# Maxima of a pair six units ahead of its exponentials instead of seven

## The reference

```python
q = (x @ Wq).reshape(B, S, 2 * H, d) * scaling      # d = 4, 2 * H = 32
scores = einsum('bhqd,bhkd->bhqk', q, k)            # causal mask, softmax over k
attn_weights = probs[:, :, 0] - lam * probs[:, :, 1]
attn = einsum('bhqk,bhkd->bhqd', attn_weights, v)   # RMS norm per head, times rms_w
x = layernorm(x + attn @ Wo)
r = sigmoid(xr @ W_r.T);  k = relu(xk @ W_k.T) ** 2 # xr, xk mix x with the row before
x = layernorm(x + r * (k @ W_v.T))
```

## Time and profile before

| | |
|---|---|
| time, median of 3 runs | 441.94 us (440.62 to 442.19) |
| profiled execution, its own time | 441.16 us |
| its span in the trace | 439.4 us |
| mean granted clock of TensorE | 0.965 |
| busy, share of the span | TensorE 90%, VectorE 90%, ScalarE 80%, GpSimd 51% |

### The profile page before, as it was taken

The page is one execution under the profiler, slowest core; times in us unless marked ns, Lnnn a source line. Parts: engine busy times, 40 slices in busy tenths (PEclk is TensorE's granted clock), DMA queues, the critical chain, the costliest instruction groups (busy, mean ns, idle before and its releaser), DMA issues.

```text
span 439.4 us, 16522 instructions
## 1 busy us (share of the span) xinstructions
PE 395.6 (90%) x5720; PEld 186.5 (42%) x5721; DVE 397.3 (90%) x565; ACT 350.9 (80%) x732; POOL 225.2 (51%) x514
## 2 busy tenths in 40 slices
PE   5846999999999999999999999999999999999882
PEld 3512444444444444444444444444444444445552
DVE  1889999999999999999999999999999999773854
ACT  2520799999999999999999999999999999787143
POOL 7300132565656565656565656565656565558412
PEclk9975599999999999999999999999999999999998
DMA  5564254321121111111111111111111110000011
GB/s 141 177 215 145 90 194 148 98 51 51 51 53 48 48 48 48 48 48 48 48 48 49 48 48 49 48 48 48 48 48 48 48 50 28 26 3 1 1 49 48
DMA packets 21390, 28.44 MB, mean 65 GB/s; under 512 B 4960, under 2 KB 9952, under 8 KB 21232
## 3 DMA queue, kind: packets, MB, share of 16 engines
q1 hardware_dynamic: 20768, 27.58, 20.9%
q10 hardware_dynamic: 592, 0.46, 0.3%
HBM read 20.39 MB, written 9.47 MB: 68 GB/s over the span
## 4 chain that ended last, share of the span: by engine, by line
PE 60%; DVE 13%; ACT 12%; issue 9%; DMA 2%; SPq 1%; POOL 1%; ACTq 1%; DVEq 0%; POOLq 0%
PE acc L677 26%; PE mx L595 13%; DVE part_max L1133 10%; ACT e_buf L1028 10%; PE ex L647 8%; PE ex L685 3%; PE mx L604 2%; PE ex L631 1%; SPq L316 1%; DMA x_tok<-in_L_attn_x 1%; PE mx L814 1%; PE mx L769 1%; PE mx L677 1%; PE ex L696 1%; POOL rs L545 1%
## 5 line engine op out<-in xcount | busy, mean ns | idle before, releaser
L1133 DVE TENSOR_REDUCE part_max<-mx 128x2 f32<-128x1024 f32 (+2 forms) x288 | 334.8, 1211 | 6.3 <-PE mx L595 2.3
L1028 ACT ACTIVATE e_buf<-ex 128x512 f32<-128x512 f32 x576 | 306.2, 601 | 36.5 <-PE ex L647 30.7
L516 POOL TENSOR_SCALAR_AFFINE_SELECT e_buf<-e_buf 128x256 f32<-128x256 f32 x256 | 100.7, 411 | 168.9 <-ACT e_buf L1028 168.7
L677 PE MATMUL acc<-e_buf,v_grp 128*32 128x256 f32 x2756 | 181.5, 352 | 4.1 <-issue 2.5
L647 PE MATMUL ex<-qe,ke 26*128 26x512 bf16 (+3 forms) x768 | 144.7, 333 | 0.7 <-ACT e_buf L1028 0.6
L595 PE MATMUL mx<-km,qm 29*128 29x128 bf16 (+3 forms) x1280 | 116.9, 270 | 12.8 <-DVE part_max L1133 10.0
L595 PEld LDWEIGHTS mx<-km,qm 26*128 26x128 bf16 (+1 forms) x1280 | 41.7, 93 | 113.8 <-DVE part_max L1133 73.5
L677 PEld LDWEIGHTS acc<-e_buf,v_grp 128*32 128x32 f32 x2756 | 64.8, 109 | 55.8 <-issue 35.5
L647 PEld LDWEIGHTS ex<-qe,ke 26*128 26x128 bf16 x768 | 45.4, 91 | 20.7 <-ACT e_buf L1028 8.2
L499 POOL TENSOR_TENSOR r_rms<-sq_eps,minus_half 128x16 f32<-128x16 f32 x15 | 43.7, 2912 | 0.1
L604 PE MATMUL mx<-mask,pick 32*128 32x128 bf16 x512 | 25.8, 220 | 0.0
(11 more groups left out here) (137 smaller groups left out, 253.6 us busy)
## 6 DMA issues: line engine op xcount, KB each, us to landing
qm<-q_rows SPq DMA_DIRECT2D x32, 128.0 KB, 2.5
km<-k_rows SPq DMA_DIRECT2D x32, 128.0 KB, 2.7
qe<-q_rows SPq DMA_DIRECT2D x32, 128.0 KB, 2.5
ke<-k_rows SPq DMA_DIRECT2D x32, 128.0 KB, 2.7
q_rows<-part_q SPq DMA_DIRECT2D x6, 256.0 KB, 3.0
k_rows<-part_k SPq DMA_DIRECT2D x6, 256.0 KB, 3.3
q_rows<-part_q SPq DMA_DIRECT2D x6, 192.0 KB
k_rows<-part_k SPq DMA_DIRECT2D x6, 192.0 KB
```

Of the source, the lines that this page charges most:

```text
L516: pool.affine_select(out=e, in_=e, compare_op=ALU.is_ge, fill=0.0, base=0, pattern=[[0, PAIR], [1, P]], channel_multiplier=-1)\
L677: last = pe.matmul(out, v, e, start=first, stop=over, skip_group_check=True)
L1028: nc.scalar.activation(e_buf[:, b, i, :], ex[:, ex_slot(b, i) % EX_BANKS, :], ACT.Exp).then_inc(s["exped"], 1)
L1133: nc.vector.tensor_reduce(target, mx_of(n, pr, m)[:].rearrange("p s (a b) -> p s a b", a=a), AX.X, ALU.max).then_inc(s["maxed"], 1)
```

## The change

The maxima of a pair begin six units ahead of its exponentials instead of seven: burst b goes with unit b + 6. The prologue does 15 units instead of 16. The transposes of the maxima move with it by one burst, from behind burst 5 to behind burst 6, in the prologue from unit `NU + 3` to `NU + 2`. In the last group the first transpose of attn, which waits for the last unit, moves from behind burst 1 to behind burst 2, on TensorE and on ScalarE. Through `m = b + EARLY`, VectorE combines at burst 3 and splits at burst 4.

```diff
-EARLY = 7
+EARLY = 6
-TAKE_AT, TURN_AT, MAXIMA_AT, INVERT_AT = 3, 7, 5, 2
+TAKE_AT, TURN_AT, MAXIMA_AT, INVERT_AT = 3, 7, 6, 2
@@ TensorE
-                if u == NU + 3:
+                if u == NU + 2:
                     turn_maxima(0, 2)
-            beside = {(0, 1): [(turn_attn, 0)], (0, 2): [(turn_attn, 1)], (0, 3): [(project, 0)],
+            beside = {(0, 2): [(turn_attn, 0), (turn_attn, 1)], (0, 3): [(project, 0)],
@@ ScalarE
-            beside = {(0, 1): [(copy_attn, 0)], (0, 2): [(copy_attn, 1)], (0, 8): [(copy_x1, 0)],
+            beside = {(0, 2): [(copy_attn, 0), (copy_attn, 1)], (0, 8): [(copy_x1, 0)],
```

## The result

The changed kernel takes 436.53 us (median of 4 runs, 436.37 to 437.08) against 442.06 us (440.62 to 442.37) for the kernel before on the same chip: a ratio of 0.9883, interval 0.987 to 0.9896. That is 5.5 us or 1.2% faster.

What follows compares the result with a forecast made beforehand. The prediction took VectorE to bind, a TensorE-ScalarE loop close behind; -0.9 (tail) + 0.2 (start) - 0.7 (transpose) + 0 (split) = -1.4 us, from the 441.94 us median to 440.5 us. The range ran from 438.0 to 446.0 us.

Steps and rivals of the forecast that it cites:

- VectorE turns only part of it into time: Loop: of some 0.2 us a pair of slack, VectorE gives back at most 1.4 us; half taken, -0.7 us.
- What bounds the kernel: Loop: VectorE binds, busy 43.35 of 43.77 us per four pairs, with a loop through TensorE and ScalarE close behind.
- Part 1: Stream of maxima: same 288 units on VectorE; if fed, the last still ends at 377.69 us, with 15 bursts left behind.
- Part 2: Tail: burst 2 done while TensorE waits for VectorE, attn's transposes side by side; -0.9 us, bounds 0 and -1.1.
- Part 3: Start: burst 0 follows prologue unit 15 instead of 16, perhaps one more burst at slow clock; +0.2 us.
- Part 4: Maxima's transpose behind burst 6: ring order gives some 0.2 us a pair of slack; -0.7 us, bounds -1.4 and +4.3.
- Part 5: Rows of maxima: DMAs land 2.5 us after first issue, a 0.05 us wait at burst 0 inside slack; bound 21 us.
- the estimated 18 us: Rows of maxima: cost if the DMA's fixed 2.0 us counted from the issue's end, about 0.6 us a pair.
- Part 6: Reciprocal behind unit 8 on VectorE: long split meets GpSimd's chain elsewhere, up to 0.27 us either way in 15 pairs; 0 taken.
- the loop relaxes and the split comes clear: Rival, 20 in 100: VectorE's waits for TensorE go (-1.4 us), long splits halve (-2 us); with tail -4 us, 438 us.
- The late maxima: Rival, 13 in 100: TensorE waits at burst 0 of each pair for the maxima's landing; +5 us (447 us) to +15 us.
- the starved VectorE: Rival, 9 in 100: transposes in two neighbouring bursts take TensorE beyond VectorE's pace; +3.4 us, 445 us.

Runs made afterwards that it cites:

- e5: Kernel before with GpSimd's normalisation of a group behind burst 7 instead of burst 2, last group unchanged: 440.78 us, ratio 0.9981.
- e8: Kernel before with VectorE's reciprocal behind burst 1 (unit 8) instead of burst 2: 440.91 us, ratio 0.9985.
- e2: Kernel before with only the first transpose of attn and its copy moved from behind burst 1 to behind burst 2: 439.72 us, ratio 0.9962.
- e1: Kernel before, lead of seven units kept, with the maxima's transpose behind burst 6 instead of 5: 447.58 us, ratio 1.0132.
- e15: Changed kernel with both attn transposes and copies behind burst 3 instead of 2, and GpSimd's normalisation behind burst 7: 437.54 us, ratio 0.9901.
- e4: Changed kernel, lead of six units kept, with the maxima's transpose back behind burst 5: 444.67 us, ratio 1.0067.
- e16: Kernel before with reciprocal behind unit 8, maxima's transpose behind the sums of burst 5, and GpSimd's normalisation behind burst 7: 439.54 us, ratio 0.9952.
- e9: Changed kernel with VectorE's reciprocal behind the combination again (burst 3 instead of burst 2): 438.91 us, ratio 0.9944.

## Why the prediction was wrong

The sum was -0.9 (tail) + 0.2 (start) - 0.7 (transpose and ring) + 0 (split) = -1.4 us. The trace shows -0.86 - 0.05 - 3.69 = -4.6 us. The step that failed is the one that capped the steady part: "VectorE turns only part of it into time", with half of 1.4 us taken and nothing for the split. Its parts in order.

**What bounds the kernel: wrong in its last step.** "VectorE binds, with a loop through TensorE and ScalarE close behind it" took for one limit what is several. I read the busy share: 43.35 of 43.77 us. But e5 took 3.1 us of splits from VectorE and the kernel gained 1.0, and e8 took VectorE out of the chain at 43.73 us a turn. A busy share of 99% didn't show the bound: most of what was taken from it came back inside the engine's own busy time.

**Part 1, the stream of maxima: wrong in its end.** The same 288 units begin at 24.51 us for 24.59, but the last one ends at 373.98 us by the next combination, and not at about 377: VectorE was fed better than before, where I had it fed equally.

**Part 2, the tail: right.** -0.86 us for -0.9, from the step named (the burst no longer stands between the transposes), and e2 shows it alone.

**Part 3, the start: +0.2 us was wrong by little.** It came to -0.05, or +0.03 counted from the first unit. The clock's slices are nearly those of before, and the waits behind the prologue add up to no loss.

**Part 4, the transpose behind burst 6: right in direction, borne out in part in its mechanism, capped wrongly.** I found 0.2 us a pair of slack in the order of ScalarE and TensorE (sums' transpose from T0 + 4.48 to 4.30). It came to T0 + 4.39 in the pair shown; behind T0 there now stands unit 1 of its pair, with 8 matmuls and 8 of the mask where unit 2 of the earlier trace rows has 2, and I had not moved it. By burst 0 it is 0.05 us in this pair, while the loop gained 0.10 us a pair, so these distances don't account for the whole. And the ring's order alone was no gain: e1, with the same transpose and the old lead, lost 0.78 us a turn. What failed is the next step, "VectorE turns only part of it into time". I let it give back only the 0.18 us of one wait, took half, and wrote -0.7 us, with -1.4 as the bound. The whole steady part gave -3.69 us in 29 pairs, 0.127 a pair: VectorE's idle time fell by 1.52 us, just past that bound, and its busy time by 2.17. I had taken the one turn of the earlier trace rows for all: the slower four pairs at the start of the loop, 44.35 us before, gave back 0.87 us, twice a turn's 0.40. The sentence that no change of order can gain more than VectorE's 3.76 idle us, unless an instruction gets shorter, held.

**Part 5, the rows of maxima: right.** Copy, issue and burst 0 came within 0.12 us of the forecast times, and burst 0 waited for no landing. The landing itself is in no record. By the start of burst 0's first matmul it was at most 196.61 - 194.16 = 2.45 us behind the first issue, so my 2.5 us was slightly long. It was also at most 196.61 - 195.36 = 1.25 us behind the end of the second, which rules out 2.0 us counted from there and with it the estimated 18 us.

**Part 6, inversion and split: wrong, a term put at nothing without working it out.** "I take 0" was -1.9 us of the splits' time. The answer stood in the trace of before, had I laid GpSimd's timeline beside VectorE's, as the last section does. Yet a shorter split alone is worth little: e5 gained 1.0 us for 3.1 of splits, and e15 got nothing for making it shorter still in the changed kernel. How much of the -3.69 us hangs on it isn't shown.

Of the rivals, "the loop relaxes and the split comes clear", to which I gave 20 in 100, comes nearest: -1.4 and -2 us there, -1.5 us of idle time and -1.9 of splits in the trace. That its two terms fit so well is partly luck, since e5 shows that a microsecond of split is not a microsecond of the kernel. It gave 438 us. Of the other 1.4 us to the median, 0.8 us is that the profiled execution of before lay below the median of 441.94 from which it was counted, and 0.6 us that the trace shows 4.6 for its 4. The range ended on that rival's own number and had no room for the spread of a median on top of it. The late maxima and the starved VectorE didn't come. In e4 VectorE is idle for 8.5 us of the steady part instead of 3.5, but through the wait for the split and not through two transposes in neighbouring bursts.

**What stays open.** The tail's 0.86 us is shown by e2. For the other 3.7 us the runs show that lead and transpose must move together, and that taking away one to three limits at lead 7 doesn't give the same; which waits make up the 3.7 us isn't shown. e16 takes three limits from lead 7 and ends at 43.64 us a turn; the changed kernel has 43.37. I could not tie the remaining 0.27 us to one wait. That the place of the reciprocal alone is worth 0.18 us in the changed kernel (e9) says that more than TensorE's order is in it. Whether the changed loop would have kept its 43.37 us with splits as long as before was not tried.

## What to carry to other kernels

When two interleaved streams are shifted against each other, count each step's place in both (bursts and units): a move that keeps one distance and shifts all else can gain where either half alone loses, and is to be costed as a whole. Where two engines are over 95% busy, a third over 90% (43.35, 42.13 and 40.31 us of 43.77), and the chain of waits goes through all of them, expect cycles of nearly the same length: a saving on one hardly shows in the time, and one move that loosens several can be worth more than the sum of the single ones (0.40 us a turn for 0.00, 0.04 and 0.04). Before an operation of 0.2 to 0.5 us whose duration varies is costed at nothing, lay the timelines of the other engines that read the same memory beside it: the variation may follow from what stands there, and then it can be forecast.

## What the hardware showed that I had not expected

The split on VectorE (L1147, two 128x16 inputs in SBUF) takes 0.16 us or up to 0.62 us, and the traces show what decides. In the kernel before, GpSimd's timeline in the pair of the long split of the earlier trace rows, which starts at 194.06 and ends at 194.49:

```profile
193.49 0.25 POOL L475 TENSOR_TENSOR r_lam<-r_den,lam_pair 128x32 f32<-128x32 f32 x1
193.82 0.63 POOL L477 TENSOR_TENSOR o_scaled<-o_tok,r_lam 128x256 f32<-128x256 f32 x1
...
195.06 0.40 POOL L485 TENSOR_TENSOR attn_sq<-attn 128x128 f32<-128x128 f32 x1
```

The product (L477) ends at 194.45. The changed kernel, VectorE's timeline:

```profile
192.22 0.25 DVE L1147 TENSOR_TENSOR turn_max<-row_max,turn_max 128x16 bf16<-128x16 f32 x1
```

and GpSimd's:

```profile
190.47 0.25 POOL L475 TENSOR_TENSOR r_lam<-r_den,lam_pair 128x32 f32<-128x32 f32 x1
...
192.04 0.40 POOL L485 TENSOR_TENSOR attn_sq<-attn 128x128 f32<-128x128 f32 x1
```

The split starts inside another, shorter instruction of the same chain and ends at 192.47, GpSimd's at 192.44. And e8, VectorE's timeline:

```profile
171.70 0.51 DVE L1147 TENSOR_TENSOR turn_max<-row_max,turn_max 128x16 bf16<-128x16 f32 x1
```

and GpSimd's:

```profile
171.55 0.63 POOL L477 TENSOR_TENSOR o_scaled<-o_tok,r_lam 128x256 f32<-128x256 f32 x1
```

Here they end at 172.21 and 172.18. In all three VectorE's short instruction ends 0.03 to 0.04 us behind the GpSimd instruction that was running when it began; with the chain elsewhere (e5) it takes 0.163 us on average over 29. The traces of all runs together hold 124 splits that began inside the product L477, and each ended 0.03 us behind it. The Trainium skill ("SBUF — State Buffer", section "Who interferes with whom") says that a VectorE instruction with two SBUF inputs contends with a GpSimd instruction that reads SBUF, that the port pair they share is an exclusive lock, and that the order of issue decides who blocks. The rows above agree. Others don't: 223 splits began inside GpSimd's power (L499, 128x16 from two inputs in SBUF, 2.91 us), and none took more than 0.19 us. So a GpSimd instruction that reads SBUF doesn't hold the split for its whole length in every case; why this one doesn't isn't shown. For the instructions of the chain above, the price of the split follows from its distance to the start of GpSimd's chain (L475), which the reciprocal releases: 194.06 - 193.49 = 0.57 us before, where the 0.63 us product stands, 192.22 - 190.47 = 1.75 us after, where a 0.40 us one does. It could have been forecast: the reciprocal moves one unit (1.13 us) away from the split, 0.57 + 1.13 = 1.70 us, and in the kernel before the instruction that runs 1.70 us behind L475 is L485, from 1.57 to 1.97 us.
